# A fused attention and convolution layer: the part behind the softmax in tiles of 128 tokens, with another route for the attention output and another prologue

## The chip, the cores and the metric

One core of a Trainium2 chip runs the whole layer in one launch. The metric is the device time of one run in microseconds (us). Three runs of the kernel before took 492.2, 495.87 and 496.88 us; their median is 495.87 us.

## The reference

Input x holds 64 samples of 64 channels by 1024 values; to the attention part each sample is 64 tokens of 1024 features. Cut to what matters:

```
h   = gelu(gelu(cond@W0+b0)@W1+b1); att = softmax(h@W2+b2)          # [64, 8]
y   = (att . weight)[b, 64, 64] @ x[b] + att@bias_k                  # mixes the 64 tokens of a sample
q   = y@Wq + bq  (32 x 32 heads);  k = y@Wk + bk;  v = y@Wv + bv     # k, v: [.., 32]
p   = softmax(q * k / sqrt(32)) per token, 32 x 32;  o = p @ v, but only [.., 32] values a token
x1  = x + o, each value of o repeated 32 times
u   = conv1d(x1, 64->64 channels, 9 taps, 4 groups, pad 4) + ctx(cond) + bias
out = x1 + u @ W4bit.T + bias
```

The reshape of the kernel uses that o is broadcast over the heads: q has to be known only as its sum over heads for the broadcast values, so Wq, Wk and Wv together give 96 columns (`w3`).

## The kernel before

The 64 samples go in 16 **units** of four (256 tokens), and a unit has two halves of 128 tokens. Per unit:

1. `project` multiplies x of the unit with `w3` (f32), ScalarE copies z to SBUF (`z_copy`), `mix` applies the mixing matrix of each sample; VectorE makes the softmax of 32 x 32 per token in `scores` and `attend`, half by half, and writes o in `divide` (L601).
2. SyncE writes o to DRAM for each half (`save_o`, L247) and, when both halves are there, reads it back eight times in the layout of the convolution, 16 partitions a time (`spread_o`, L254), in pieces of 32 values (128 bytes).
3. GpSimd adds it to the convolution's input (`add_o`: three instructions for each of four channel groups, L327, L328, L330), ScalarE takes the upper part in the reduced f32 format (`c_high`, L410), GpSimd the rest (`c_low`, L336). TensorE makes the convolution of a group with six matmuls of 512 columns (`conv`, L709).
4. ScalarE adds the bias (`u_copy`, L419), TensorE transposes (`transpose_u`), ScalarE and VectorE split again (`u_high`, L427; `u_low`, L605).
5. `linear` multiplies with the 4-bit weights: 64 matmuls of 512 columns a unit, in 16 slots of four. VectorE adds x1 (`finish`, L613; x1 comes from GpSimd's `residual`), SyncE stores.

Each engine runs a list written out by hand and waits on semaphores. In iteration i TensorE makes `linear` of unit i-2 and, in fixed slots between, `conv` and `transpose_u` of unit i-1, and `project` and `mix` of unit i+1. ScalarE, VectorE, GpSimd and SyncE have their own lists in the same iterations. Everything that SyncE issues goes through one queue, in order.

Ahead of the loop lies a prologue: a small network gives `att`; 64 matmuls with 24 rows make the mixing matrices (L784; the weights are split in two parts by VectorE L483, L486 and GpSimd L306); sums over the heads give `w3` (L514); units 1 to 4 are projected ahead (`NZ` = 5). The projection of unit 0 is L794, column sums are L798.

Of the kernel before, what the change touches and what calls it, by code (L numbers as in the profile page):

```python
# [13 lines left out]
P = 128  # L14
# [8 lines left out]
UT = UB * S  # L23
NU = B // UB
NT = NU * TU
SLOTS = 16
# [11 lines left out]
for _name, _n in (("cond", B), ("w0", P), ("w1", P), ("w2", KE), ("b0", 1), ("b1", 1), ("cbias", G), ("part", 1),  # L38
                  ("scale", 1), ("zero", 1), ("b2", KE), ("mixb", P), ("brow", W3)):
    AT[_name] = slice(NCOLS, NCOLS + _n)  # L40
    NCOLS += _n


def block_program(nc, xt_in, xc_in, cols, mix_w, wq, wvk, conv_w, ctx_w, packed_t, xn_in, bias_in, out):
    ctx = ExitStack()
    with ctx:
# [15 lines left out]
        xc = sb("xc", [P, 2, UB, G, MW])  # L62
        c_hi = sb("c_hi", [P, UB, G, MW], F32R)
# [11 lines left out]
        o_sb = sb("o_sb", [P, 2, TU, DH])  # L75
        o_c = sb("o_c", [P, 2, UB, G, DH])
        u_sb = sb("u_sb", [P, 2, UB * P])
# [15 lines left out]
        cond_sb, w0_sb, w1_sb, w2_sb, b0_sb, b1_sb, cbias_sb, part_sb, sc, zero, b2_all, mixb_all, brow_all = (  # L93
            cols_sb[:, at] for at in AT.values())
        b2_sb = b2_all[0:B, :]
        mixb_sb = mixb_all[0:2 * KE, :]
        brow_sb = brow_all[0:NH, :]
        h_sb = sb("h_sb", [P, 2, B])
        att = sb("att", [B, 3, KE])
        att_s = sb("att_s", [B, 4])  # L100
        att_r = sb("att_r", [B, 4, DH], F32R)
        att_t = sb("att_t", [P, B], F32R)
        mix_bias = sb("mix_bias", [P, NT])
        u_bias = sb("u_bias", [P, G, B])
        zp = sb("zp", [P, 5])
# [6 lines left out]
        mixw = prob[:, 0, :, :].rearrange("p d e -> p (d e)")  # L112
        mixw_hi = c_hi[:, :, :, :].rearrange("p n g m -> p (n g m)")[:, 0:D]
        mixw_r = c_lo[:, :, :, :].rearrange("p n g m -> p (n g m)")[:, 0:2 * D].rearrange("p (s h i) -> p s h i", h=2, i=S)
# [25 lines left out]

        o_dram = nc.dram_tensor("o_dram", [NU, UT, DH], F32).ap()

# [22 lines left out]
        s_mwh = sem("s_mwh")  # L165
        s_mwr = sem("s_mwr")
        s_mwd = sem("s_mwd")
# [8 lines left out]
        s_zp = sem("s_zp")  # L176
        s_flag = sem("s_flag")
# [19 lines left out]
        s_x1 = sem("s_x1")  # L197
# [13 lines left out]
        def ut_view(t, b, g):  # L211

            return t[:, b % 2, :, :].rearrange("p r (n g c) -> p g n r c", n=UB, g=G)[:, g, :, :, :]


        NI = NU + 3

        Z_SLOT = (1, 6)
        CONV_SLOT = (3, 5, 8, 10)
        UT_SLOT = (7, 9, 11, 12)  # L220
        MIX_SLOT = 13
# [3 lines left out]
        def _(eng):  # L225
# [10 lines left out]
            def load_c(u):  # L236
                if u >= 2:
                    eng.wait_ge(s_cl, G * (u - 1))
                eng.dma_start(xc[:, u % 2, :, :, :], xc_in[u]).then_inc(s_xc[u % 2], 16)

            def store(d, t):
                eng.wait_ge(s_res, 4 * d + 2 * t + 2)
                eng.dma_start(out[d, t], xn[:, d % NXN, t, :]).then_inc(s_out[d % NXN], 16)

            def save_o(a, t):
                eng.wait_ge(s_o, TU * a + t + 1)
                eng.dma_start(o_dram[a, t * P:(t + 1) * P, :], o_sb[:, a % 2, t, :]).then_inc(s_ow, 16)  # L247
# [16 lines left out]
            eng.dma_start(cw[:, :, :, :], conv_w).then_inc(s_cw, 16)  # L264
            load_c(0)
            eng.dma_start(ctx_sb[:, :, :], ctx_w).then_inc(s_ctx, 16)
            eng.wait_ge(s_w3[0], 1)
            load_x(1)
            load_x(2)
            load_c(1)  # L270
            for u in range(3, NZ):
                load_x(u)
            eng.dma_start(bias_n[:, :], bias_in).then_inc(s_bias, 16)

            for i in range(NI):
                a, d = i, i - 2
                if 0 <= d - 1 < NU:
                    store(d - 1, 1)
                if NZ <= i + 2 < NU:
                    load_x(i + 2)  # L280
                if a < NU:
                    save_o(a, 0)
                if 2 <= i + 1 < NU:
                    load_c(i + 1)
                if a < NU:
                    save_o(a, 1)
                    spread_o(a)
# [10 lines left out]
        def _(eng):  # L298
            eng.memset(att_r[:, :, :].bitcast(F32), 0.0).then_inc(s_zero, 1)
# [5 lines left out]
            eng.wait_ge(s_mwr, 1)  # L305
            eng.tensor_copy(mixw_r[:, :, 1, :], mixw_r[:, :, 0, :].bitcast(F32)).then_inc(s_mwd, 1)  # L306
# [9 lines left out]
            def add_o(b, g):  # L316


                x4 = xc[:, b % 2, :, g, 1:MW].rearrange("p n (d j) -> p n d j", j=4)
                x0 = xc[:, b % 2, :, g, 0:P].rearrange("p n (d j) -> p n d j", j=4)  # L320
                o = o_c[:, b % 2, :, g, :]
                if g == 0:
                    eng.wait_ge(s_xc[b % 2], 16 * (b // 2 + 1))
                    eng.wait_ge(s_oc[b % 2], 16 * R * (b // 2 + 1))  # L324
                else:
                    eng.wait_ge(s_add, 3 * (G * b + g))
                eng.tensor_tensor(x4[:, :, :, 0:3], x4[:, :, :, 0:3], o.unsqueeze(3).broadcast_to([P, UB, DH, 3]), ALU.add).then_inc(s_add, 1)  # L327
                eng.tensor_tensor(x4[0:64, :, :, 3], x4[0:64, :, :, 3], o[0:64], ALU.add).then_inc(s_add, 1)  # L328
                eng.wait_ge(s_add, 3 * (G * b + g) + 1)
                eng.tensor_tensor(x0[64:P, :, :, 0], x0[64:P, :, :, 0], o[64:P], ALU.add).then_inc(s_add, 1)  # L330

            def c_low(b, g):
                eng.wait_ge(s_add, 3 * (G * b + min(g + 2, G)))
                eng.wait_ge(s_ch, G * b + g + 1)
                eng.wait_ge(s_conv, G * (b - 1) + g + 1)
                eng.tensor_tensor(c_lo[:, :, g, :], xc[:, b % 2, :, g, :], c_hi[:, :, g, :].bitcast(F32), ALU.subtract).then_inc(s_cl, 1)  # L336

            def residual(b, t):
                if t == 0:
                    eng.wait_ge(s_add, 3 * G * (b + 1))  # L340
                    eng.wait_ge(s_xn[b % NXN], 16 * (b // NXN + 1))
                    if b == 0:
                        eng.wait_ge(s_bias, 16)
                x = xn[:, b % NXN, t, :]
                runs = x.rearrange("p (d e) -> p d e", d=DH)
                eng.wait_ge(s_o, TU * b + t + 1)
                eng.tensor_tensor(runs, runs, o_sb[:, b % 2, t, :].unsqueeze(2).broadcast_to([P, DH, D // DH]), ALU.add).then_inc(s_x1, 1)  # L347
                eng.wait_ge(s_x1, 4 * b + 2 * t + 1)
                eng.tensor_tensor(x, x, bias_n[:, :], ALU.add).then_inc(s_x1, 1)  # L349

            for b in range(NU):
                add_o(b, 0)
                add_o(b, 1)
                if b:
                    c_low(b, 0)
                add_o(b, 2)
                if b:
                    c_low(b, 1)
                add_o(b, 3)
                if b:  # L360
                    c_low(b, 2)
                    c_low(b, 3)
                residual(b, 0)
                residual(b, 1)
# [3 lines left out]
        def _(eng):  # L368
            for n, bias in enumerate((b0_sb, b1_sb)):
                eng.wait_ge(s_pe0, n + 1)  # L370
                eng.activation(h_sb[:, n, :], p_sm[0][:, 64 * n:64 * n + 64], ACT.Gelu, bias=bias).then_inc(s_act0, 1)
            eng.wait_ge(s_att, 3)
            eng.activation(att[:, 1, :], att[:, 0, :], ACT.Exp, accum_out=att_s[:, 2:3]).then_inc(s_act0, 1)
            for m in range(8):
                eng.wait_ge(s_mixed, m + 1)
                for h in range(2):
                    rows = slice(h * S, h * S + S)
                    eng.activation(mix_t[rows, :, 8 * m:8 * m + 8].rearrange("p t s -> p s t"),
# [517 lines left out]
```

## Time and profile before

| | |
|---|---|
| Median of three runs | 495.87 us (492.2 to 496.88) |
| Profiled execution | 494.59 us |
| Its span, first to last instruction | 492.8 us |
| Busy in the span: TensorE, VectorE, ScalarE, GpSimd | 450.7, 333.2, 228.3, 346.8 us |
| Instructions | 7038 |
| Moved by DMA | 79.78 MB in 55522 packets, 41904 of them under 512 bytes |

All durations below come from the one profiled execution. A matmul in f32 leaves two records, one in the reduced format leaves one. Records of matmuls overlap, so their cost is read from start to start, not from their length.

### The profile page before, as it was taken

The page shows a single profiled execution, that of the slowest core. Times are in us where ns is not written, and L with a number is a line of the kernel's source. Part 1 is how long each engine was busy: PE and PEld are TensorE (multiplying, and loading weights), DVE is VectorE, ACT ScalarE, POOL GpSimd, SP SyncE. Part 2 cuts the span into 40 slices and gives each one's busy share as a digit, 9 for nine tenths or more (in the row PEclk, how much of TensorE's full clock was granted, in tenths as well). Part 3 has the DMA queues.
Part 4 walks back from the last instruction along what each step waited for, and adds up shares of the span by engine and source line. Part 5 has one row for each costly group of instructions (what it writes and reads, how often), then busy time and mean ns, then how long its engine had stood idle before and what let it go on. Part 6 is the DMA issues. An engine that isn't in the chain of part 4 may idle for free. (4 is left out here: it accounts for less than half of the span.)

```text
span 492.8 us, 7038 instructions
## 1 busy us (share of the span) xinstructions
PE 450.7 (91%) x2403; PEld 373.5 (76%) x2403; DVE 333.2 (68%) x532; ACT 228.3 (46%) x458; POOL 346.8 (70%) x329
## 2 busy tenths in 40 slices
PE   3998272999999999999999999999999999997996
PEld 2998151777877888888888888787888888775885
DVE  4639685739793968677785949495968678692121
ACT  2705570546354545545463645454544535472520
POOL 2400493969697968797696969697869788696920
PEclk9999596799999999999999999999999999999999
DMA  8956324254555556473827464546547352606112
GB/s 338 413 212 217 106 89 108 65 132 184 139 224 142 221 133 235 116 252 97 269 97 214 149 171 161 150 175 163 200 116 252 106 178 93 190 4 189 47 44 85
DMA packets 55522, 79.78 MB, mean 162 GB/s; under 512 B 41904, under 2 KB 41904, under 8 KB 50864
## 3 DMA queue, kind: packets, MB, share of 16 engines
q1 hardware_dynamic: 55472, 79.08, 49.7%
q8 instruction: 35, 0.57, 0.5%
q14 instruction: 15, 0.12, 0.1%
HBM read 61.76 MB, written 17.30 MB: 160 GB/s over the span
## 5 line engine op out<-in xcount | busy, mean ns | idle before, releaser
L725 PE MATMUL p_f<-w_ffn,u_lo 128*128 128x512 f32 x512 | 204.1, 399 | 0.0
L725 PE MATMUL p_f<-w_ffn,u_hi 128*128 128x512 f32 x512 | 202.2, 405 | 1.1 <-DVE u_lo L605 1.1
L419 ACT ACTIVATE u_sb<-p_conv,u_bias,cols_sb 128x128 f32<-128x128 f32 x256 | 96.2, 457 | 59.9 <-PE p_conv L709 59.0
L327 POOL TENSOR_TENSOR xc<-xc,o_c 128x384 f32<-128x384 f32 x64 | 56.7, 886 | 92.2 <-DMA o_c<-o_dram 90.8
L725 PEld LDWEIGHTS p_f<-w_ffn,u_hi 128*128 128x128 f32 x512 | 97.0, 189 | 21.2 <-issue 1.3
L725 PEld LDWEIGHTS p_f<-w_ffn,u_lo 128*128 128x128 f32 x512 | 97.1, 190 | 18.3
L613 DVE TENSOR_TENSOR xn<-p_f,xn 128x512 f32<-128x512 f32 x64 | 44.0, 688 | 84.5 <-PE p_f L725 84.5
L336 POOL TENSOR_TENSOR c_lo<-xc,c_hi 128x516 fp32r<-128x516 f32 x60 | 78.3, 1310 | 9.7 <-issue 6.2
L410 ACT ACTIVATE c_hi<-xc 128x516 fp32r<-128x516 f32 x64 | 40.8, 638 | 87.6 <-POOL xc L330 87.5
L349 POOL TENSOR_TENSOR xn<-xn,bias_n 128x1024 f32<-128x1024 f32 x32 | 77.1, 2408 | 2.5
L709 PE MATMUL p_conv<-c_hi,cw_hi 128*128 128x512 f32 x128 | 53.6, 419 | 26.0 <-POOL c_lo L336 14.6
L605 DVE TENSOR_TENSOR u_lo<-p_ut,u_hi 128x512 fp32r<-128x512 f32 x64 | 43.9, 689 | 33.0 <-ACT u_hi L427 32.9
L347 POOL TENSOR_TENSOR xn<-xn,o_sb 128x1024 f32<-128x1024 f32 x32 | 61.7, 1928 | 0.1
L709 PE MATMUL p_conv<-c_lo,cw_hi 128*128 128x512 f32 x128 | 52.5, 410 | 0.0
L709 PE MATMUL p_conv<-c_hi,cw_lo 128*128 128x512 f32 x128 | 52.4, 410 | 0.0
L709 PEld LDWEIGHTS p_conv<-c_hi,cw_hi 128*128 128x128 f32 x128 | 24.9, 194 | 35.4 <-issue 29.6
L427 ACT ACTIVATE u_hi<-p_ut 128x512 fp32r<-128x512 f32 x64 | 38.6, 603 | 26.6 <-PE p_ut L720 25.2
L404 ACT ACTIVATE prob<-prob 128x1024 f32<-128x1024 f32 x32 | 34.0, 1062 | 30.3 <-DVE prob L580 30.3
L686 PEld LDWEIGHTS p_sm<-w,xt 128*128 128x128 f32 x384 | 46.3, 191 | 1.8
L686 PE MATMUL p_sm<-w,xt 128*128 128x96 f32 x384 | 46.0, 273 | 0.0
L584 DVE TENSOR_REDUCE den<-prob 128x32 f32<-128x1024 f32 x32 | 38.7, 1210 | 7.3 <-ACT prob L404 7.3
L592 DVE TENSOR_REDUCE p_sm<-prob 128x32 f32<-128x1024 f32 x32 | 39.3, 1228 | 1.1
(99 smaller groups left out, 502.5 us busy)
## 6 DMA issues: line engine op xcount, KB each, us to landing
xc<-xc_in_in SPq DMA_DIRECT2D x16, 1032.0 KB, 5.0
xt<-xt_in_in SPq DMA_DIRECT2D x16, 1024.0 KB, 7.6
xn<-xn_in_in SPq DMA_DIRECT2D x16, 1024.0 KB, 6.0
out<-xn SPq DMA_DIRECT2D x32, 512.0 KB, 6.5
o_c<-o_dram SPq DMA_DIRECT2D x128, 32.0 KB, 2.1
xn<-wq_in SPq DMA_DIRECT2D x3, 1024.0 KB, 10.6
xt<-wq_in SPq DMA_DIRECT2D x1, 1024.0 KB, 6.5
prob<-mix_w_in SPq DMA_DIRECT2D x1, 512.0 KB, 4.4
```

Source lines behind the costliest of these rows:

```text
L327: eng.tensor_tensor(x4[:, :, :, 0:3], x4[:, :, :, 0:3], o.unsqueeze(3).broadcast_to([P, UB, DH, 3]), ALU.add).then_inc(s_add, 1)
L336: eng.tensor_tensor(c_lo[:, :, g, :], xc[:, b % 2, :, g, :], c_hi[:, :, g, :].bitcast(F32), ALU.subtract).then_inc(s_cl, 1)
L347: eng.tensor_tensor(runs, runs, o_sb[:, b % 2, t, :].unsqueeze(2).broadcast_to([P, DH, D // DH]), ALU.add).then_inc(s_x1, 1)
L349: eng.tensor_tensor(x, x, bias_n[:, :], ALU.add).then_inc(s_x1, 1)
L410: eng.activation(c_hi[:, :, g, :], xc[:, b % 2, :, g, :], ACT.Copy).then_inc(s_ch, 1)
L419: ins = eng.activation(u_sb[:, g % 2, n * P:(n + 1) * P], p_conv[g % 2][:, n * P:(n + 1) * P], ACT.Identity, bias=u_bias[:, g, UB * b + n: ...
L592: eng.tensor_reduce(num(a)[:, t, :], prob[:, t, :, :], AX.X, ALU.add).then_inc(s_num, 1)
L605: eng.tensor_tensor(ut_view(u_lo, b, g), p_ut[g % 2][:, :].rearrange("p (n r c) -> p n r c", n=UB, r=R), ut_view(u_hi, b, g).bitcast(F32), ...
L613: eng.tensor_tensor(x, p_f[q % 2][:, :], x, ALU.add).then_inc(s_res, 1)
L686: last = mm(z_ps(a)[:, t * W3:(t + 1) * W3], xt[:, a % NXT, r, t * P:(t + 1) * P], w3[:, r, :], start=(r == 0), stop=(r == R - 1))
L709: last = mm(p_conv[g % 2][:, :], w[:, k, g, :], src[:, :, g, k:k + P], start=(n == 0), stop=(n == 5))
L725: return mm(p_f[half][:, :], u[:, d % 2, r, t * P:(t + 1) * P], w_ffn[:, r, 512 * half:512 * half + 512], **flags)
```

## The change

A **tile** k is half a unit: 128 tokens, two samples; there are 32, and two of them share a buffer of a unit.

- Behind the softmax everything goes by tiles: `add_o`, `c_high`, `c_low`, `conv`, `u_copy`, `transpose_u`, `u_high`, `u_low`, `linear`, `finish`. `conv` has six matmuls of 256 columns (48 a unit, not 24), `transpose_u` two transposes and not four, `linear` the same matmuls as before in 8 slots a tile.
- VectorE writes o four times over (`o_sb` [.., 32, 4]); `save_o` and `spread_o` run once a tile, and the spread moves runs of 128 values (512 bytes), shifted by one column for the first 64 partitions. `add_o` becomes one instruction a group. There are 256 issues of `spread_o`, not 128, of 64 KB and not 32.
- The mixing matrices come from plain f32: 128 matmuls with 8 rows, on four groups of 32 rows, and no split on VectorE and GpSimd. ScalarE's queue loads their weights (4 DMAs).
- The prologue's order is another: column sums between the projections of unit 0 chunk by chunk, `u_bias` on ScalarE, weights of the linear part converted in four pieces, `keep_busy` matmuls of a matrix of ones (6, three times 4, and 16).
- GpSimd adds the bias and o to x in the other order (`x_bias`, `x_o`), and makes `c_low` of unit 0 too.

In the diff the loops over `NU + 2`, `NT + 1`, `NT` and `NT` are those of SyncE, GpSimd, ScalarE and VectorE, in this order.

```diff
-SLOTS = 16
+SLOTS = 8
-        o_sb = sb("o_sb", [P, 2, TU, DH])
+        o_sb = sb("o_sb", [P, 2, TU, DH, 4])
+        def conv_slot(k, g):
+            return SLOTS * k - 8 + g if k < 6 else SLOTS * k - 12 + 2 * g
+        def ut_slot(k, g):
+            return SLOTS * k - 6 + g if k < 6 else SLOTS * k - 9 + 2 * g
+        PROJ = {2 * SLOTS * (a - 3) + 3 + 4 * t: (a, t) for a in range(NZ, NU) for t in range(TU)}
+        MIX = {2 * SLOTS * (a - 3) + 13: a for a in range(3, NU)}
...
             def spread_o(k):
+                t = k % TU
+                eng.wait_ge(s_ow, 16 * (k + 1))
...
                 for r in range(R):
+                    at = 1 if r < PAD else 0
+                    eng.dma_start(o_c[r * CG:(r + 1) * CG, TN * t:TN * t + TN, :, at:at + P].rearrange("c n g m -> c (n g) m"),
+                                  o_dram[k].rearrange("(q c) m -> c q m", c=CG)).then_inc(s_oc[t], 16)
...
+            for i in range(NU + 2):
+                if 0 <= 2 * i - 4 < NT:
+                    store(2 * i - 4)
+                if 2 <= i < NU:
+                    load_c(i)
+                if 1 <= i < NU:
...
+                    load_n(i)
+                if i < NU:
+                    save_o(2 * i)
+                    spread_o(2 * i)
+                    save_o(2 * i + 1)
+                    spread_o(2 * i + 1)
...
+                x = rows_of(xc[:, (k // TU) % 2, :, :, :], k, g)
+                eng.tensor_tensor(x, x, rows_of(o_c, k, g), ALU.add).then_inc(s_add, 1)
...
+            for k in range(NT + 1):
+                if k < NT:
+                    add_o(k, 0)
+                    add_o(k, 1)
+                    c_low(k, 0)
+                    add_o(k, 2)
+                    c_low(k, 1)
+                    add_o(k, 3)
+                    c_low(k, 2)
+                    c_low(k, 3)
+                if k >= 1:
+                    if k >= 3:
+                        x_bias(k - 1)
+                    x_o(k - 1)
...
+            for k in range(NT):
+                a, t = k // TU + 1, k % TU
+                nxt = k + 1 < NT
+                if t == 0 and 2 <= a < NU:
+                    exp(a, 0)
+                u_copy(k, 0)
+                c_high(k, 3)
+                u_copy(k, 1)
+                u_high(k, 0)
+                if t == 0 and a < NU:
+                    exp(a, 1)
+                if nxt:
+                    c_high(k + 1, 0)
+                u_copy(k, 2)
...
+            for k in range(NT):
+                a, t = k // TU + 2, k % TU
+                A, N = a < NU, k + 1 < NT
+                if k:
+                    finish(k - 1, 1)
+                if N:
+                    u_low(k + 1, 0)
+                if A and t == 0:
+                    softmax_top(a)
+                    score(a, 0)
+                if A and t == 1:
+                    sum_exp(a, 0)
+                    times_v(a, 0)
+                if N:
+                    u_low(k + 1, 1)
+                if A and t == 0:
+                    subtract(a, 0)
+                if A and t == 1:
+                    sum_v(a, 0)
+                    divide(a, 0)
+                finish(k, 0)
...
+            def keep_busy(bank, n):
+                for _ in range(n):
+                    mm(bank[:, 0:P], ones[:, :], ones[:, :], start=True, stop=True)
...
+            for n in range(CG):
+                for j in range(4):
+                    rows = slice(32 * j, 32 * j + KE)
+                    for h in range(2):
+                        last = mm(p_mixed[j][h * S:h * S + S, NT * n:NT * n + NT], mixw[rows, n, :], att_t[rows, h::2], start=True, stop=True)
...
+            keep_busy(p_f[1], 16)
+            conv(0, 0)
...
+            for s in range(SLOTS * NT):
+                linear(s // SLOTS, s % SLOTS)
+                if s in TRANS:
+                    k, g = TRANS[s]
+                    transpose_u(k, g)
+                if s in CONV:
+                    k, g = CONV[s]
+                    conv(k, g)
```

**Where instructions moved.** TensorE in the middle of the loop. Before, a group's convolution between two slots of `linear`, and its transposes (L709, L720; L725 is `linear`):

```order
L709 MATMUL p_conv<-c_hi,cw_hi 128x512 [waits s_cl,s_u]
L709 MATMUL p_conv<-c_lo,cw_hi 128x512
L709 MATMUL p_conv<-c_hi,cw_lo 128x512
L709 MATMUL p_conv<-c_hi,cw_hi 128x512
L709 MATMUL p_conv<-c_lo,cw_hi 128x512
L709 MATMUL p_conv<-c_hi,cw_lo 128x512
L725 MATMUL p_f<-w_ffn,u_hi 128x512
L725 MATMUL p_f<-w_ffn,u_lo 128x512
L725 MATMUL p_f<-w_ffn,u_hi 128x512
L725 MATMUL p_f<-w_ffn,u_lo 128x512
L720 MATMUL p_ut<-ident,u_sb 128x128 [waits s_ul,s_u]
L720 MATMUL p_ut<-ident,u_sb 128x128 x3
```

Now the same place of the list (L722, L731; L736 is `linear`):

```order
L722 MATMUL p_conv<-c_hi,cw_hi 128x256 [waits s_cl,s_u]
L722 MATMUL p_conv<-c_lo,cw_hi 128x256
L722 MATMUL p_conv<-c_hi,cw_lo 128x256
L722 MATMUL p_conv<-c_hi,cw_hi 128x256
L722 MATMUL p_conv<-c_lo,cw_hi 128x256
L722 MATMUL p_conv<-c_hi,cw_lo 128x256
L736 MATMUL p_f<-w_ffn,u_hi 128x512
L736 MATMUL p_f<-w_ffn,u_lo 128x512
L736 MATMUL p_f<-w_ffn,u_hi 128x512
L736 MATMUL p_f<-w_ffn,u_lo 128x512
L731 MATMUL p_ut<-ident,u_sb 128x128 [waits s_ul,s_u]
L731 MATMUL p_ut<-ident,u_sb 128x128
```

A group comes twice as often, with half the columns and half the transposes; its waits come twice as often too.

ScalarE in the loop. Before, the upper parts of the next unit (L410, c_hi) stand in a block ahead of the copies of u (L419) of the same unit:

```order
L410 ACTIVATE c_hi<-xc 128x4x129 [waits s_conv,s_add] x2
L404 ACTIVATE prob<-prob 128x1024 [waits s_sub]
L410 ACTIVATE c_hi<-xc 128x4x129 [waits s_conv,s_add]
L419 ACTIVATE u_sb<-p_conv,u_bias,cols_sb 128x128 [waits s_ut,s_conv]
L419 ACTIVATE u_sb<-p_conv,u_bias,cols_sb 128x128 x3
```

Now c_hi (L421) of tile k+1 stands between the copies (L429) and the upper parts (L437) of tile k:

```order
L429 ACTIVATE u_sb<-p_conv,u_bias,cols_sb 128x128 [waits s_ut,s_conv]
L429 ACTIVATE u_sb<-p_conv,u_bias,cols_sb 128x128
L437 ACTIVATE u_hi<-p_ut 128x2x8x16 [waits s_f,s_ut]
L421 ACTIVATE c_hi<-xc 128x2x129 [waits s_conv,s_add]
L429 ACTIVATE u_sb<-p_conv,u_bias,cols_sb 128x128 [waits s_ut,s_conv]
L429 ACTIVATE u_sb<-p_conv,u_bias,cols_sb 128x128
L437 ACTIVATE u_hi<-p_ut 128x2x8x16 [waits s_f,s_ut]
L421 ACTIVATE c_hi<-xc 128x2x129 [waits s_conv,s_add]
```

So a wait for `add_o` of the next tile now stands ahead of the third and fourth `u_copy` of this one.

## Rows read from the trace of the kernel before

**Rows 1.** The page, parts 1 and 2: busy us, share, instructions; slices in tenths

```profile
PE 450.7 (91%) x2403; PEld 373.5 (76%) x2403; DVE 333.2 (68%) x532; ACT 228.3 (46%) x458; POOL 346.8 (70%) x329
...
PEclk9999596799999999999999999999999999999999
...
GB/s 338 413 212 217 106 89 108 65 132 184 139 224 142 221 133 235 116 252 97 269 97 214 149 171 161 150 175 163 200 116 252 106 178 93 190 4 189 47 44 85
```

**Rows 2.** Waits of TensorE from 60 us on: us in total, times, longest

```profile
PE p_conv L709 <- POOL c_lo L336: 14.6, 3, 10.6
```

**Rows 3.** Timeline of TensorE, 0 to 75 us: start, us, engine, line, names

```profile
11.26 2.96 PE L784 MATMUL p_ut<-att_t,c_lo 24*128 24x64 f32 x13
...
22.54 6.21 PE L794 MATMUL p_conv<-w,xt 128*128 128x96 f32 x32
28.58 1.95 PE L798 MATMUL p_sm<-w,ones 128*128 128x96 f32 x16
31.37 0.55 PE L697 MATMUL p_sm<-z_sb,mix_t 64*64 64x96 f32 x8 [0.83 <-ACT z_sb L396]
...
32.78 3.76 PE L686 MATMUL p_sm<-w,xt 128*128 128x96 f32 x32
...
58.80 0.76 PE L709 MATMUL p_conv<-c_hi,cw_hi 128*128 128x512 f32 x1 [10.05 <-DVE c_lo L617]
...
72.70 0.47 PE L725 MATMUL p_f<-w_ffn,u_hi 128*128 128x512 f32 x1 [1.14 <-DVE u_lo L605]
```

**Rows 4.** Timeline of TensorE, 74 to 115 us

```profile
87.43 0.77 PE L709 MATMUL p_conv<-c_hi,cw_hi 128*128 128x512 f32 x1 [10.60 <-POOL c_lo L336]
```

**Rows 5.** The chain that ended last: start us, us, what

```profile
441.11 1.41 DMA o_dram<-o_sb
...
446.66 2.29 DMA o_c<-o_dram
...
454.59 2.90 PE p_conv L709 x6
...
459.25 1.46 PE p_conv L709 x6
460.71 2.08 PE p_f L725 x9
...
489.08 0.69 DVE xn L613
```

**Rows 6.** Timeline of VectorE, 0 to 110 us

```profile
6.42 1.29 DVE L486 SCALAR_TENSOR_TENSOR c_lo<-c_hi,cols_sb,prob 128x1024 fp32r<-128x1024 f32 x1
...
32.53 0.23 DVE L561 TENSOR_TENSOR k_sb<-p_sm,qkv_bias 128x64 f32<-128x64 f32 x1
...
42.57 0.19 DVE L601 TENSOR_TENSOR o_sb<-p_sm,rden 128x32 f32<-128x32 f32 x1
...
46.76 0.19 DVE L601 TENSOR_TENSOR o_sb<-p_sm,rden 128x32 f32<-128x32 f32 x1
...
96.93 0.19 DVE L601 TENSOR_TENSOR o_sb<-p_sm,rden 128x32 f32<-128x32 f32 x1
```

**Rows 7.** Timeline of GpSimd, 0 to 120 us

```profile
107.34 0.89 POOL L327 TENSOR_TENSOR xc<-xc,o_c 128x384 f32<-128x384 f32 x1 [3.47 <-DMA o_c<-o_dram]
```

**Rows 8.** Groups by line and shape: busy us, mean ns; idle before

```profile
L419 ACT ACTIVATE u_sb<-p_conv,u_bias,cols_sb 128x128 f32<-128x128 f32 x256 | 96.2, 457 | 59.9 <-PE p_conv L709 59.0
L336 POOL TENSOR_TENSOR c_lo<-xc,c_hi 128x516 fp32r<-128x516 f32 x60 | 78.3, 1310 | 9.7 <-issue 6.2
...
L327 POOL TENSOR_TENSOR xc<-xc,o_c 128x384 f32<-128x384 f32 x64 | 56.7, 886 | 92.2 <-DMA o_c<-o_dram 90.8
...
L605 DVE TENSOR_TENSOR u_lo<-p_ut,u_hi 128x512 fp32r<-128x512 f32 x64 | 43.9, 689 | 33.0 <-ACT u_hi L427 32.9
L410 ACT ACTIVATE c_hi<-xc 128x516 fp32r<-128x516 f32 x64 | 40.8, 638 | 87.6 <-POOL xc L330 87.5
...
L330 POOL TENSOR_TENSOR xc<-xc,o_c 64x128 f32<-64x128 f32 x64 | 33.7, 526 | 4.8
```

More of the change, by code:

```diff
@@ L156, in block_program @@
         s_ow = sem("s_ow")
-        s_oc = [sem(f"s_oc{i}") for i in range(2)]
+        s_oc = [sem(f"s_oc{t}") for t in range(TU)]
         s_ident = sem("s_ident")
@@ L351, in _ @@
[L351 to L364, printed above, removed]
+                    eng.wait_ge(s_xc[(k // TU) % 2], 16 * (k // (2 * TU) + 1))
+                    eng.wait_ge(s_oc[k % TU], 16 * R * (k // TU + 1))
@@ L438, in _ @@
+            convert_weights(1, 0)
+            exp(0, 1)
+            convert_weights(1, 1)
+            for a in range(1, NZ):
+                z_copy(a)
+            eng.wait_ge(s_ub, G)
+            c_high(0, 0)
             exp(1, 0)
-            c_high(0, 0)
-            exp(1, 1)
             c_high(0, 1)
-            u_copy(0, 0)
             c_high(0, 2)
-            u_copy(0, 1)
-            u_high(0, 0)
-            c_high(0, 3)
-            u_copy(0, 2)
-            u_high(0, 1)
-            u_copy(0, 3)
@@ new lines, in _ @@
+            for k in range(NT):
[19 more added lines that the diff above has]
+                finish(k, 0)
+                if N:
+                    u_low(k + 1, 2)
+                if A and t == 0:
+                    score(a, 1)
+                if A and t == 1:
+                    sum_exp(a, 1)
+                    times_v(a, 1)
+                if N:
+                    u_low(k + 1, 3)
+                if A and t == 0:
+                    subtract(a, 1)
+                if A and t == 1:
+                    sum_v(a, 1)
+                    divide(a, 1)
@@ L735, in linear, with product, open_bank @@
-            def linear(d, slot):
-                q, n = slot // 4, slot % 4
+            def product(k, half, r, u, **flags):
+                t = k % TU
+                return mm(p_f[half][:, :], u[:, (k // TU) % 2, r, t * P:(t + 1) * P], w_ffn[:, r, 512 * half:512 * half + 512], **flags)
+            def open_bank(k, half):
+                if k:
+                    eng.wait_ge(s_res, 2 * k + half - 1)
+                product(k, half, 0, u_hi, start=True, stop=False)
+            def linear(k, slot):
+                half, n = slot // 4, slot % 4
@@ L760, in linear @@
-                if n == 3 and q == 1:
-                    open_bank(d, 2)
+                        product(k, half, r, u_lo, start=False, stop=True).then_inc(s_f, 1)
             eng.wait_ge(s_small, 16)
@@ L807, in _ @@
             last.then_inc(s_cb, 1)
-            for a in range(1, NZ):
+            for a in range(2, NZ):
                 for t in range(TU):
```

543 lines of the change are left out of this document (228 added, 315 removed).

## The prediction, made before the changed kernel had run

> **What bounds the kernel now.** I read the page first, then TensorE's timeline, its waits, and the chain. The page shows TensorE busy for 450.7 us of 492.8, VectorE for 333.2, GpSimd for 346.8 [rows 1]. From 87 us on TensorE hardly waits: the loop is bound by the matmuls. What is not matmul lies at three places. Ahead of the loop: the first convolution comes at 58.80, the first matmul of `linear` at 72.70 [rows 3]. A hole of 10.60 us before 87.43, where TensorE waits for GpSimd's `c_low` of unit 1 [rows 4]. One of about 3.4 us near the end, of the same kind (14.6 us in three waits) [rows 2]. The chain shows what lies behind such a wait: o saved, spread, added on GpSimd, split, then `conv` at 454.59 [rows 5]. After a hole the granted clock is at its lower level, 1.2 GHz (the slices with 5, 9, 6 [rows 1]): six matmuls of a convolution take 2.90 us there, 1.46 us at 2.4 GHz [rows 5].
>
> The profiled run took 494.59 us, 1.8 more than its span; the median of the three is 1.3 above it. I sum the span and carry both over.
>
> **The change part by part: until the softmax of unit 0 starts** (k_sb at 32.53 [rows 6]). The mixing matmuls start at 11.26 [rows 3], after VectorE has been held by the splitting (6.42 to 7.7 [rows 6]). Without that, `att` is ready 2 us earlier: start 9.2. They took 11.3 us (to 22.54). Now 128 f32 matmuls make 256 passes. Bounds: all 64-column weight loads one after the other at 1.2 GHz; the 16 passes of L798, each with a load of 128 columns, took 1.95 us at the higher level, .12 each [rows 3]; 64 columns at half the clock take about as much, 256 x .11 = 28 us. Or four row groups side by side, a quarter of that: 7 us. `mix`, whose halves lie on two row groups, makes eight passes of 64 columns in .55 us, .069 each at 2.4 GHz [rows 3]; with four groups at 1.2 GHz the same per pass or somewhat less. I take 10 us, near the low end, as that row has row groups too: end 19.2. Then 48 passes of unit 0 and column sums, and 24 of `keep_busy`. Passes with 128-column weights took 6.21/32 = .194 in L794 and 3.76/32 = .117 in L686 [rows 3]: the clock rose in between. 72 passes are 8.4 us at the one, 14 at the other level; before, 48 took 8.0. I take 10: 29.2, then 1.2 to the softmax, as before less the bias that is now made earlier: **start at 30.4**, 2.1 earlier.
>
> **From there to the first `linear`** (before: 72.70-32.53 = 40.2). Times from the softmax's start. o of tile 0 is ready at 10.3 (42.76), of tile 1 at 14.5 (46.95) [rows 6]. Before, the spread waited for both. Now tile 0 goes at once: save 1.4, eight issues 3.9, landing 2.3 [rows 5], 2.5 us of waiting behind `load_x(4)`, issued just before (1 MB at the 413 GB/s of the busiest slice [rows 1]), and .3, my guess for twice the bytes: o lands at 20.7. `add_o` was 886 ns for 384 elements, `c_low` 1310 for 516 [rows 8]: about 2.2 ns an element over .2 us, so .75 each for 258. `c_low(0,0)` ends at 23. TensorE itself comes at 25: three projections of .113 x 32 = 3.6 us, each behind its load, then 16 `keep_busy`, 3.6. Then the groups pass through ScalarE: `u_copy` .75 (96.2 us over 256, two each), `c_high` .4 (638 ns for 516 elements) [rows 8], two `exp` of 1.05, in an order in which `c_high(1,g)` of tile 1 stands between. o of tile 1 lands at 26, as its save waits for tile 0's eight issues; GpSimd, through with `c_low(0,3)` at 27.8, adds it by 28.6. Stepwise on ScalarE: `c_high(1,0)` 29.5, `u_copy(0,2)` 30.2, `u_copy(0,3)` 31.7, last `u_high` 32.9, and VectorE's `u_low` 33.3. **`linear` starts at 33.4**, 6.8 sooner; in all at 63.8 instead of 72.70.
>
> **The loop.** Before: 489.08-72.70 = 416.4 us [rows 3, 5]. Off: holes 14.6 [rows 2] and matmuls at half clock, 11 x .2 + 1.44 = 3.6. That leaves 398.2. Added:
> - Conv: a 512-column matmul takes 1.46/6 = .243 [rows 5], of which 512/2.4 GHz is .213, so .03 besides. With 256 columns: .107+.03 = .137; `linear`'s .231 (2.08 us for nine) gives .124. I take .130: 48 x .130 - 24 x .243 = +.41 a unit, 15 units: **+6**. Over the 744 conv matmuls of tiles 1 to 31 the bounds are .113 (L686's 32 starts spread over 3.6 us, weights of 128 columns and a short stream), -12.6; and .22 (L686's pass and a 256-column stream in turn), +67.
> - Tile 1's convolution and transposes lie now behind the first `linear`: 24 x .13 + 8 x .11 (a pass of L686) = **+4**.
> - Transposes: as many as before, side by side with nothing lost in a switch: 0.
> - New waits. `u_copy(k,2)` stands behind `c_high(k+1,0)`. Early on, tiles 2 and 4 arrive late for it: o of tile 2 is divided at 31.7 (behind `u_low(0,1)`, 31.05), plus 8.5 for save and spread (as above, with no load ahead) 40.2, plus add, upper part and copy 42.1; the transposes are due at 40, after four slots of 1.42 (.92 of `linear`, half a conv group's .78, .11). **+2.2**. Tile 4: `u_low(2,0)` after slot 10 of `linear`, 51.9, then `attend` (4.2, as from 42.57 to 46.76 [rows 6]): divided 56.4, copy ready 66.8, due 64.9: **+2**. Tile 6 is just in time. Later see rival C. With 1.8 for the last units, whose slots are shorter: **+6** in all.
> - VectorE: u_low 128 x .42 instead of 43.9, the wider o .1 x 32: +13 us, to about 346. GpSimd: one add of .75 replaces 886 and two of about 530 ns, -28; `c_low` +18. Both stay below 85% and hide behind TensorE.
> - SyncE: 128 more issues of .45 and a dozen MB more; the queue idles for most of a unit. 0, but see C.
>
> Loop 398.2+6+4+6 = 414.2, and 3.7 from 489.08 to the end for the last add and store, as before. **Span 30.4+33.4+414.2+3.7 = 481.7**, run 483.5, against a median 484.8: I say **484.5**.
>
> **A rule against the change.** The rows first. In L686 load and stream of 96 columns take .117 together [rows 3], and the stream is .04 of it (96/2.4 GHz) if each column takes a cycle, .08 if two; so a load of 128 columns takes .04 to .08 of its own at least, and in turn with 512 columns' .213 it would make .25 to .29. The nine `linear` matmuls, each with a fresh weight, take .231 [rows 5]: the load hides. The Trainium skill ("TensorE: Matmul & The Clock Gate", "The mechanism" in Part 3) says that a weight load overlaps running matmuls only when its row group differs. By that rule load and stream of a conv matmul come in turn; taken from the rows, that is the .22 above at most, and 484.5+67 = 551. The rows contradict it; chance .02. The same page ("Back-to-back issue gap") gives 262 cycles for 256 columns, .109 us; it would make 484.5-16 = 469, the far end of A below. Its 518 cycles for 512 (.216) are less than this trace's .231 and .243.
>
> **The rivals.**
> A, 476: tiles arrive in time everywhere (-4) and conv goes at the .124 of the `linear` row (-4.5). For it: the two stalls of 2 us hang on sums of a dozen terms, in which I put each transfer behind its longest neighbour. Against: `c_high` stands where it does. Chance .24.
> B, 497: the mixing matmuls don't run side by side. At two groups' pace they take 18 to 28 us, not 10, and the whole prologue follows, +8 to +18. Against: `mix` shows two at a time. Chance .12.
> C, slower, 508: each even tile j. VectorE can divide its o only after `u_low(j-2,1)`, whose transposes come in slot 8j-23; `u_copy(j-1,2)`, behind `c_high(j,0)`, must be ready for slot 8j-13. Ten slots are 10 x 4 x .231 + 5 convolutions of .78 + transposes 1.1 + a projection 1.8 + `mix` .55 = 16.6 us. In them must pass 2.9 (split, sum, divide), save to arrival, and 1.95 (add, `c_high`, `u_copy`): room for 11.7 us. Save to arrival was 7.8 in the chain (441.11 to 448.95 [rows 5]) and 10.2 (97.12 to 107.34 [rows 6, 7]). Now it has twice the bytes and stands behind a store and two loads, 2.5 MB. From 11.7 on every us is paid in 13 units: at 13.5, 1.8 x 13 = +23. Chance .14.
> Weight loads in turn: 551, .02. The forecast, 478 to 491: .48.
>
> **The numbers.** A measurement of this kernel can tell about 1%, 491 to 501 around 495.87. Faster by over 1%: nearly all of the forecast (.46) and A (.24) = .70. Within: B and the forecast's rest, .14. Slower: C and the loads, .16. The range reaches from A's low end, 473, to where C begins, 499: it leaves out C, the loads and little of A.
>
> **What would show it.** The first `linear` matmul at 64 us, not 73; no hole of 10 us after it, but two of about 2; conv matmuls .124 to .137 apart; mixing matmuls over in about 10 us; the o transfer within 11.7 us of `divide`. Wrong if TensorE waits for u_sb in every second tile, if the mixing takes over 15 us, or if the conv matmuls are .15 or more apart.

## The result: 25.7% slower, not 2% faster

The changed kernel took **621.78 us** (median of four runs, 619.83 to 623.82) beside 494.93 us for the kernel before on the same chip. The ratio is 1.257, its 95% interval 1.249 to 1.265. The profiled span is 620.6 us, the forecast was 481.7. Forecast, range and sign were wrong. One rival (C) had the kernel slower, at 508 us by a late o; none names what happened.

First the page of the changed kernel, parts 1, 2 and 6 (engine, busy us, share, instructions; the slices; then the DMA issues with KB each and median us to landing). It answers to [rows 1].

```profile
PE 486.8 (78%) x3047; PEld 421.0 (68%) x3047; DVE 329.5 (53%) x584; ACT 227.9 (37%) x579; POOL 330.4 (53%) x333
...
PEclk9989898987969979698796977969879698899999
...
o_c<-o_dram SPq DMA_DIRECT2D x256, 64.0 KB, 2.6
```

GpSimd is down from 346.8 to 330.4 us and VectorE is near its old value: no engine has become the bound. But TensorE is busy for 78% only, and its clock falls again and again over the whole run, where before it stayed up from the ninth slice on. Next, what TensorE waits for from 60 us on (us in total, times, longest), against the single line of [rows 2]:

```profile
PE p_sm L699 <- DMA xt<-xt_in_in: 95.6, 11, 9.7
PE p_sm L710 <- ACT z_sb L410: 7.7, 11, 0.8
PE p_ut L731 <- ACT u_sb L429: 7.2, 6, 2.0
PE p_f L736 <- DVE u_lo L608: 6.0, 5, 1.9
```

`project` waits for x in 11 places, units 5 to 15, each time nearly 9 us. One of them, on SyncE's queue (start, us, line, names):

```profile
314.50 0.33 SPq L260 DMA_DIRECT2D o_dram<-o_sb  x1
316.93 3.64 SPq L271 DMA_DIRECT2D o_c<-o_dram  x8
320.61 0.43 SPq L260 DMA_DIRECT2D o_dram<-o_sb  x1
323.19 4.92 SPq L271 DMA_DIRECT2D o_c<-o_dram  x8
328.15 0.43 SPq L256 DMA_DIRECT2D out<-xn  x1
328.62 0.43 SPq L241 DMA_DIRECT2D xt<-xt_in_in  x1
344.24 0.34 SPq L256 DMA_DIRECT2D out<-xn  x1
```

and on TensorE (the first projection of that unit, and the second, 16 passes each):

```profile
334.23 3.73 PE L699 MATMUL p_sm<-w,xt 128*128 128x96 f32 x16 [8.71 <-DMA xt<-xt_in_in]
...
343.53 1.92 PE L699 MATMUL p_sm<-w,xt 128*128 128x96 f32 x16
```

TensorE is ready for x at 334.23 - 8.71 = 325.52. SyncE issues the load only at 328.62, as its list now has `load_x(i + 2)` as the last thing of an iteration, behind both tiles' `save_o` and `spread_o` and a store. In the kernel before it was the second thing of an iteration, behind one store and ahead of both saves; the bullets on the change don't list this move. x can be used 5.6 us after the issue. 3.1 late + 5.6 = 8.7 us. And the 16 passes behind the hole take 3.73 us, the 16 a little later 1.92: TensorE comes out of the hole at the lower clock, 1.2 GHz (granted .50 from 334 to 338 us). The stretches of 20 us of the same trace (busy us of TensorE, granted clock, DMA share, GB/s):

```profile
320.00:340.00 20.00, 11.29 (x59) 0.74 0.39 120
340.00:360.00 20.00, 19.30 (x121) 1.00 0.47 165
```

### The profile page after: what moved, and what is told of

It reads as the page before. It is cut to its first block and busy times, and to the rows that moved or that the text cites. A ratio compares the mean times of both kernels' runs of the same rounds, so it can differ in the third digit from the quotient of the medians.

```text
span 620.6 us, 9085 instructions
## 1 busy us (share of the span) xinstructions
PE 486.8 (78%) x3047; PEld 421.0 (68%) x3047; DVE 329.5 (53%) x584; ACT 227.9 (37%) x579; POOL 330.4 (53%) x333
## 5 line engine op out<-in xcount | busy, mean ns | idle before, releaser
L344 POOL TENSOR_TENSOR c_lo<-xc,c_hi 128x258 fp32r<-128x258 f32 x128 | 95.4, 745 | 236.8 <-ACT c_hi L421 232.7
L736 PE MATMUL p_f<-w_ffn,u_hi 128*128 128x512 f32 x512 | 208.2, 417 | 6.0 <-DVE u_lo L608 6.0
L736 PE MATMUL p_f<-w_ffn,u_lo 128*128 128x512 f32 x512 | 209.4, 410 | 0.0
L608 DVE TENSOR_TENSOR u_lo<-p_ut,u_hi 128x256 fp32r<-128x256 f32 x128 | 53.7, 420 | 241.3 <-ACT u_hi L437 240.4
L699 PE MATMUL p_sm<-w,xt 128*128 128x96 f32 x384 | 66.0, 344 | 95.6 <-DMA xt<-xt_in_in 95.6
L437 ACT ACTIVATE u_hi<-p_ut 128x256 fp32r<-128x256 f32 x128 | 49.6, 388 | 195.6 <-PE p_ut L731 195.0
L429 ACT ACTIVATE u_sb<-p_conv,u_bias,cols_sb 128x128 f32<-128x128 f32 x256 | 102.9, 457 | 46.6 <-PE p_conv L722 46.6
L736 PEld LDWEIGHTS p_f<-w_ffn,u_hi 128*128 128x128 f32 x512 | 99.1, 194 | 21.0 <-DVE u_lo L608 6.5
L736 PEld LDWEIGHTS p_f<-w_ffn,u_lo 128*128 128x128 f32 x512 | 100.7, 197 | 12.5
L338 POOL TENSOR_TENSOR xc<-xc,o_c 128x258 f32<-128x258 f32 x128 | 93.8, 744 | 18.0 <-DMA o_c<-o_dram 18.0
L421 ACT ACTIVATE c_hi<-xc 128x258 fp32r<-128x258 f32 x128 | 54.7, 427 | 104.6 <-POOL xc L338 104.6
L722 PE MATMUL p_conv<-c_hi,cw_hi 128*128 128x256 f32 x256 | 75.2, 294 | 0.0
L722 PE MATMUL p_conv<-c_lo,cw_hi 128*128 128x256 f32 x256 | 73.8, 288 | 0.0
L722 PE MATMUL p_conv<-c_hi,cw_lo 128*128 128x256 f32 x256 | 73.5, 287 | 0.0
L731 PE MATMUL p_ut<-ident,u_sb 128*128 128x128 f32 x256 | 50.0, 277 | 7.5 <-ACT u_sb L429 7.4
L722 PEld LDWEIGHTS p_conv<-c_hi,cw_hi 128*128 128x128 f32 x256 | 50.3, 196 | 5.6
L731 PEld LDWEIGHTS p_ut<-ident,u_sb 128*128 128x128 f32 x256 | 35.3, 142 | 27.1 <-ACT u_sb L429 10.9
L722 PEld LDWEIGHTS p_conv<-c_lo,cw_hi 128*128 128x128 f32 x256 | 50.0, 195 | 5.2
```

Of the source, the lines that this page charges most:

```text
L338: eng.tensor_tensor(x, x, rows_of(o_c, k, g), ALU.add).then_inc(s_add, 1)
L344: eng.tensor_tensor(rows_of(c_lo, k, g), rows_of(xc[:, (k // TU) % 2, :, :, :], k, g), rows_of(c_hi, k, g).bitcast(F32), ALU.subtract).the ...
L421: eng.activation(rows_of(c_hi, k, g), rows_of(xc[:, (k // TU) % 2, :, :, :], k, g), ACT.Copy).then_inc(s_ch, 1)
L429: ins = eng.activation(u_sb[:, g % 2, n * P:(n + 1) * P], p_conv[g % 2][:, n * P:(n + 1) * P], ACT.Identity, bias=u_bias[:, g, bat:bat + 1 ...
L437: eng.activation(ut_view(u_hi, k, g), p_ut[g % 2][:, 0:TN * P].rearrange("p (n r c) -> p n r c", n=TN, r=R), ACT.Copy).then_inc(s_uh, 1)
L608: eng.tensor_tensor(ut_view(u_lo, k, g), p_ut[g % 2][:, 0:TN * P].rearrange("p (n r c) -> p n r c", n=TN, r=R), ut_view(u_hi, k, g).bitcas ...
```

## The experiments

Two theories of the 127 us. **T1**: the place of `load_x` in SyncE's list. **T2**: o's transfers, of four times the bytes, crowd the queue or the memory, so that x comes late wherever it is issued. (Expectations name them so.)

**x_early: the load of x at the head of the iteration.**

```diff
             for i in range(NU + 2):
+                if NZ <= i + 2 < NU:
+                    load_x(i + 2)
                 if 0 <= 2 * i - 4 < NT:
                     store(2 * i - 4)
...
-                if NZ <= i + 2 < NU:
-                    load_x(i + 2)
```

> The changed kernel with one edit: SyncE issues load_x(i+2) at the head of iteration i, ahead of the store, not at its end. Theory 1, the place in the queue: in the changed kernel the load is issued behind both spreads and lands 8 to 9.7 us after TensorE wants it, in each of 11 units. Then the edit takes away the 95.6 us of waiting and the matmuls at half clock behind them (about 25 us): 480 us, between 474 and 490. Theory 2, the transfers of o crowd the DMA queue with four times the bytes, so that x is late wherever it is issued: the wait moves or shrinks by less than half, 560 us or more, or o becomes late in its stead.

Measured: 499.48 us beside 494.74, ratio 1.010 (1.007 to 1.013), span 495.8. TensorE's waits from 60 us on, the one for x gone:

```profile
PE p_sm L710 <- ACT z_sb L410: 7.7, 11, 0.8
PE p_ut L731 <- ACT u_sb L429: 7.3, 7, 2.0
PE p_f L736 <- DVE u_lo L608: 6.0, 5, 1.9
```

Moving one DMA a unit is worth 122.3 us. That is T1; but the expectation for the kernel without this fault was 480, at most 490, and it still lies 1% on the wrong side of the kernel before.

**x_mid: the load between the two halves' o.** The same two lines behind `spread_o(2 * i)`, ahead of `save_o(2 * i + 1)`.

> The same load between the two halves of the o transfer (behind spread_o(2i), ahead of save_o(2i+1)). Theory 1: it is issued about 5 us earlier than in the changed kernel, at the end of the first spread, and lands at about the time that TensorE wants it: 480 to 500 us, and o of the odd tiles 2 to 3 us later at no cost, since they have room. Theory 2: as with the load early, over 560 us.

Measured: 500.39 us, ratio 1.014 (1.007 to 1.022); TensorE waits 2.1 us for x in five places, at most .9. The edge lies here: the load may stand behind one half's o, not behind both.

**before_x_late: the kernel before, with the changed kernel's place of the load** (behind `spread_o` and `store(d, 0)`).

> The kernel before with only the place of the load changed as in the change: load_x(i+2) at the end of SyncE's iteration, behind spread_o and store. Theory 1: there it is issued at about slot 13 of 16, lands 7 us later, and is wanted in slot 1 of the next iteration: 1 to 3 us late in each of 11 units, 10 to 35 us slower, 505 to 530 us. Theory 2 (bytes): the spread has its old bytes, so no change, 495 us.

Measured: 562.41 us, ratio 1.138 (1.131 to 1.145). Its trace:

```profile
PE p_sm L686 <- DMA xt<-xt_in_in: 41.2, 11, 8.1
PE p_conv L709 <- POOL c_lo L336: 12.1, 2, 8.7
```

Here o moves as it did before, in 128 pieces of 32 KB, and the same 11 waits come in, one of 8.1 us and ten of 2.8 to 4.3. T2 isn't needed. Nor is x's load slower beside o's larger transfers: the loads of x land 6.8 us after their issue in the changed kernel (median), 9.1 us here. The waits of the changed kernel are longer because more of the list lies ahead of the load: from the first save of an iteration to the load 14.1 us there (314.50 to 328.62), 10.7 here (220.07 to 230.77).

The late load cost 68 us where I had expected at most 35: the waits for x are 41.2 of it, so some 27 us are something else. The granted clock is .918 instead of .971. Times the spans that is 46.1 - 14.3 = 32 us of full-speed time, an estimate and an upper one, as TensorE idles for a part of it: enough for the rest.

**after_no_x: the changed kernel without the x loads of units 5 to 15** (old data is projected; the 11 MB are not moved).

```diff
-                if NZ <= i + 2 < NU:
-                    load_x(i + 2)
...
-                    eng.wait_ge(s_x[a % NXT], 16 * (a // NXT + 1))
+                    eng.wait_ge(s_x[a % NXT], 16 * (min(a, NZ - 1 - (NZ - 1 - a) % 2) // NXT + 1))
```

> The changed kernel without the x loads of units 5 to 15; it leaves out these transfers (11 MB) and projects old data, all else as it is. Theory 1: the time without any wait for x, 478 us, within 1% of the early load. Theory 2: if the o transfers themselves are late for the convolution, some of the loss stays: over 500 us.

Measured: 497.18 us in one run, span 495.4, against the early load's 495.8. As far as one run can tell, an early x costs nothing, by its bytes or its place. Theory 1's 478 us did not come in: what is left above it has another cause than x.

### What the idle holes cost beside their length

The span fell by 124.8 us with the early load, the waits for x were 95.6; 29.2 us are left. **after_fill** has 70 extra matmuls in each hole, on the changed kernel with its late load:

```diff
                 if t == 0:
+                    if a >= NZ:
+                        eng.wait_ge(s_o, TU * (a - 1))
+                        keep_busy(z_ps(a), 70)
                     eng.wait_ge(s_x[a % NXT], 16 * (a // NXT + 1))
```

> The changed kernel with its late x load, and 70 extra f32 matmuls of ones (128 columns, into the bank that the projection then overwrites) ahead of project's wait for x in units 5 to 15: TensorE stays busy in the hole of about 9 us. Their results are not used. At the .11 us a pass of the row of transposes 70 of them fill about 7.7 us of it. Theory 1 (the stretch at 1.2 GHz comes from the idle hole, and costs 20 to 29 us in all 11 units beside the 95.6 of waiting): the lower level behind the holes goes, and the time falls from 622 to 593 to 603 though more work is done. Rival (the clock would fall there anyway, or its fall costs nothing that the next wait for x doesn't take back): 615 to 625.

Measured: 670.05 us, at a granted clock of .986 instead of .89. Both ranges were missed, as I had taken a matmul of ones for one pass. It leaves two:

```profile
305.65 15.79 PE L689 MATMUL p_sm<-ones 128*128 128x128 f32 x140
321.29 1.92 PE L702 MATMUL p_sm<-w,xt 128*128 128x96 f32 x16
```

15.6 us are more than the hole, and TensorE never waits for x. So **fill_36** has 36 of them.

> As the run with 70 extra matmuls ahead of the late x of units 5 to 15, but 36 of them. The 70 were two passes each, .112 us apart (112 records in 12.51 us), 15.7 us a unit, more than the hole; its span was the early load's 495.8 and 11 x 15.7 = 172.7 more, 668.5 (669.1 measured), at a granted clock of .986. 36 fill 8.1 of the 8.7 us that TensorE waits on average: 88.7 of the 95.6. Theory 1 (the lower clock comes from the idle hole): only waits are filled, so no time is added, and what the stretches at 1.2 GHz cost, about 29 us, goes: span 591 to 595, a median of 593 to 599, with TensorE executing 396 extra matmuls. Rival (the clock costs nothing of its own, the holes are only longer or shorter with it): 620 to 624.

Measured: **594.24 us** (591.63 to 595.5), span 593.7. Waits, and the stretch that answers to the one above:

```profile
PE p_ut L734 <- ACT u_sb L429: 8.5, 8, 2.0
PE p_sm L713 <- ACT z_sb L410: 7.7, 11, 0.8
PE p_sm L702 <- DMA xt<-xt_in_in: 6.6, 6, 1.8
```

```profile
320.00:340.00 20.00, 19.22 (x132) 1.00 0.48 179
```

396 matmuls whose results nobody reads make the kernel 27.5 us faster. x is as late as before, and the clock stays nearly always at its upper level, 2.4 GHz (granted .99 from 100 to 460 us, against .85). Of the span's 26.9 us (620.6 - 593.7) 1.6 lie ahead of the first `linear` (65.02 against 63.40), so 25.3 come from the loop; x_early gives 29.2 for the same thing. So the 127 us over the kernel before are: waits for x 95.6, the clock's fall behind them 25 to 29, and 2 to 6 that have to do with neither.

### The rest: two places in ScalarE's list

At x_early's `mix` TensorE waits for `z_copy` once a unit. ScalarE's timeline of that kernel shows why (start, us, line, names, idle before):

```profile
150.04 0.38 ACT L437 ACTIVATE u_hi<-p_ut 128x256 fp32r<-128x256 f32 x1 [1.72 <-PE p_ut L731]
150.32 0.32 ACT L410 ACTIVATE z_sb<-p_sm 128x192 f32<-128x192 f32 x1
```

The copy stands behind the last `u_high`, which waits for transposes that TensorE has just issued, right ahead of `mix`. **z_early** puts it in front of `u_copy(k, 3)`; **chigh_late** moves the two `c_high` behind `u_copy`; **both** does both:

```diff
+                u_copy(k, 2)
                 if nxt:
                     c_high(k + 1, 0)
-                u_copy(k, 2)
                 u_high(k, 1)
+                if t == 0 and NZ <= a + 1 < NU:
+                    z_copy(a + 1)
+                u_copy(k, 3)
                 if nxt:
                     c_high(k + 1, 1)
-                u_copy(k, 3)
                 u_high(k, 2)
                 if nxt:
                     c_high(k + 1, 2)
                 u_high(k, 3)
-                if t == 0 and NZ <= a + 1 < NU:
-                    z_copy(a + 1)
```

> The early x load, and ScalarE's z_copy of the next unit put ahead of u_copy(k,3) instead of at the end of the unit's list, behind u_high(k,3). In the profile with the x load early TensorE waits 7.7 us in 11 places at mix for that z_copy. Theory 1 (the copy stands behind u_high, which waits for transposes that TensorE issues in the slot of mix itself): those 7.7 us go, and the time falls from 499.5 to 492, range 489 to 495; the waits for u_sb and u_lo stay at 7 and 6 us. Rival (the waits change place, as u_copy is now behind z_copy, .3 us later): u_sb's wait grows by 5 us or more and the time stays within 2 us of 499.5.

Measured: 495.07 us beside 494.02, ratio 1.002 (1.000 to 1.005). The 7.7 us at `mix` are gone, but u_sb's wait grew:

```profile
PE p_ut L731 <- ACT u_sb L429: 10.7, 14, 2.0
PE p_f L736 <- DVE u_lo L608: 6.7, 6, 1.9
```

Theory and rival each had a half: of the 7.7 us, 3.4 came back at u_sb and .7 at u_lo, and the time lies just outside the range of the one (489 to 495) and the condition of the other.

> The early x load, and on ScalarE c_high(k+1,0) behind u_copy(k,2) and c_high(k+1,1) behind u_copy(k,3), each one place later than in the changed kernel. TensorE waits 7.3 us at the transposes for u_sb, which u_copy writes. Theory 1 (u_copy is late because c_high of .43 us waits ahead of it for VectorE or for the addition): the 7.3 us of u_sb and part of the 6.0 us of u_lo behind it go, and the time falls from 499.5 to 492 to 496. Rival (u_copy waits for the convolution, or c_high, later now, holds up c_low and the next convolution): a new wait of TensorE at conv for c_hi or c_lo of 5 us or more, and a time from 499 to 506.

Measured: 495.52 us, ratio 1.005 (1.004 to 1.007). The time is within theory 1's range, but u_sb's wait only fell by half, to 3.9 us in four places, and u_lo's rose to 7.4. The rival's new wait of 5 us didn't come; `conv` waits .5 us for u_sb.

> Both edits of ScalarE's list on top of the early x load. If the two waits are independent the gains add up: 499.5 less 7.7 less 4 to 7 is 485 to 488, range 483 to 492, under the kernel before by 1 to 2%. Rival (one wait stands behind the other, and VectorE's finish and u_low set the pace of the unit): no more than the better of the two alone, 490 to 493.

Measured: **487.53 us** beside 494.02, ratio .989 (.987 to .991), span 485.5. The gain of 12.0 us on x_early is more than the two alone (4.4 and 4.0). x_early ran on another chip; by the ratios, each to its own kernel before, the gains are 2.1% against .8 and .5%, so this holds. The waits behave alike: 8.5 us less in all, against 3.6 and 1.5. It fits that with `c_high` out of the way the early `z_copy` no longer pushes `u_copy` back (u_sb's wait is 4.0 us, not 10.7), but no run tests this reason by itself:

```profile
PE p_f L736 <- DVE u_lo L608: 7.4, 6, 2.2
PE p_ut L731 <- ACT u_sb L429: 4.0, 5, 1.1
PE p_conv L722 <- ACT u_sb L429: 1.1, 3, 0.6
```

### The keep_busy matmuls

> The early x load, and none of the keep_busy matmuls (6 ahead of the mixing, 4 at three places between the sums of Wq, 16 ahead of the first convolution). Theory 1 (they fill waits and hold nothing up): the lower clock of 1.2 GHz comes in for 3 to 7 us at one or two more places of the first 60 us, and the time is 0 to 4 us over 499.5. Rival (they lie on the path themselves): 1 to 3 us less than 499.5.

Measured: 493.50 us, ratio 1.001 (.999 to 1.004), runs from 492.63 to 497.03. That is 6.0 us under x_early, on another chip, where at most 3 had been expected. Not all of it is in the trace: in the profiled execution (496.91 us) the first `linear` comes at 62.36 instead of 65.33, but the span is only .7 us shorter, 495.1. The first matmuls of the loop run at the lower clock (granted .52 from 61 to 68 us, against .85 in x_early), as theory 1 had said they might, and the waits in the loop are 1.1 us longer. With so wide a spread this decides nothing, so the next runs take them out of `both`, with `both` beside it on the same chip.

> Early x load, both edits of ScalarE's list, and no keep_busy matmuls. In the run with the x load early, taking them out gave 493.5 against 499.5, of which the two batches' spread may be a part. If they lie on the path: 482 to 486. If that difference was chance: 487 to 489, as with both edits alone.

> Early x load and both edits of ScalarE's list once more, for a closer ratio to the kernel before: 487 to 488.5, ratio .986 to .991.

Measured: both_nb **482.19 us** (ratio .979, .976 to .982), both_again 487.14 us (.988, .985 to .990). The first `linear` matmul of each, both_again first:

```profile
65.70 0.47 PE L736 MATMUL p_f<-w_ffn,u_hi 128*128 128x512 f32 x1 [1.36 <-DVE u_lo L608]
```

```profile
59.78 0.47 PE L736 MATMUL p_f<-w_ffn,u_hi 128*128 128x512 f32 x1 [1.37 <-DVE u_lo L608]
```

They hold the prologue up by 5.9 us, and the span of 485.7 falls to 479.4. The 68 passes take 10.9 us in all, so they lie on the path for about half of their time: the twelve ahead of the mixing (which starts at 9.4 without them, 10.5 with them), the eight ahead of a chunk of Wq (three times) and the 32 ahead of the first convolution stand where less than their length was being waited for. Rows of both_again:

```profile
28.35 1.08 PE L689 MATMUL p_sm<-ones 128*128 128x128 f32 x8
...
54.24 3.84 PE L689 MATMUL p_f<-ones 128*128 128x128 f32 x32
57.83 0.36 PE L722 MATMUL p_conv<-c_hi,cw_hi 128*128 128x256 f32 x1
```

In both_nb the first convolution starts at 51.58, after a wait of 1.77 us for `c_lo`; here the clock doesn't fall behind it (granted 1.00 from 61 to 75 us). This is the fastest version: the change, the load at the head, ScalarE's two moves, and no keep_busy, 2.1% under the kernel before.

## Why the prediction was wrong, step by step

**The step that failed is the bullet on SyncE in the loop**, "128 more issues of .45 and a dozen MB more; the queue idles for most of a unit. 0". It counts the issues that are added and not the one that is moved: `load_x(i + 2)`, from the head of the iteration to its end. A queue that idles for most of a unit still holds an issue until the one ahead is allowed. In the unit shown the save of the even tile waits 7.0 us for `divide`, until 314.50. From there the list is a chain: save, landing, eight issues of `spread_o`, and the same for the odd tile, 14.1 us until the load goes out; the odd tile's own `divide` (over at 319.88) is not waited for. The term put at 0 cost 95.6 us of waits and 25 to 29 us of clock. I compared o's path with its due slot (rival C) and never x's with slot 3 of `project`. What it left out can be read off the changed kernel: TensorE ready at 325.52, the spread over at 328.11, the load issued at 328.62 and of use 5.6 later, 8.7 us, 11 times. I also gave the fall of the clock behind a hole no term for a hole that recurs, though [rows 1, 5] show it.

Rival C looked at the right engine for the wrong transfer. With x early, o of an even tile is saved at 231.11, its eight spreads end at 236.31 and land 2.6 later: 7.8 us, under the 11.7 that it had room for. C didn't come in. Nor did any of the prediction's signs of being wrong come in: they look at u_sb, the mixing and the conv matmuls, none at x.

**Until the first linear: right**, 65.02 against 63.8 (before 72.70).

- Mixing matmuls, taken as 10 us from 9.2: they start at 10.42, behind twelve passes of ones that the sum left out, and the last at 18.4. Eight us, of which 4.11 are one idle stretch that no semaphore explains:

```profile
17.59 0.33 PE L790 MATMUL p_f<-att_t,prob 8*64 8x32 f32 x4 [4.11 <-issue]
```

  So the four row groups do run side by side, faster than the low bound of 7 us without that stretch; B was wrong. The stretch comes behind 200 of the 256 passes here and in x_early, and behind 212 in both_nb and no_busy, where the twelve passes of ones ahead of the mixing are gone: each time at the same place of TensorE's list of instructions, whatever the time. What TensorE lacks there isn't shown.
- Softmax of unit 0 (`k_sb`) at 31.42, forecast 30.4, and 33.6 us from there, forecast 33.4. keep_busy was counted in the sum and never asked what it bought: taken out of `both`, it gives 5 us, more than the whole error of this part.
- `add_o` was taken as .75, measured 744 ns; `c_low` .75, 745 ns; `u_low` .42, 420 ns.

**The loop**, taken as 414.2. With x early it is 492.10 (the last `finish`) - 65.33 = 426.8, 12.6 more:

- Conv, taken as .130 a matmul: .120, as in these rows of the changed kernel:

```profile
57.52 0.28 PE L722 MATMUL p_conv<-c_hi,cw_lo 128*128 128x256 f32 x1
57.64 0.28 PE L722 MATMUL p_conv<-c_hi,cw_hi 128*128 128x256 f32 x1
57.75 0.29 PE L722 MATMUL p_conv<-c_lo,cw_hi 128*128 128x256 f32 x1
57.88 0.29 PE L722 MATMUL p_conv<-c_hi,cw_lo 128*128 128x256 f32 x1
```

  The other side of the term was off as well: a conv matmul before, taken as .243, is .237 (four of them take .95 us, from 201.82 to 202.77, in the kernel before). With .120 and .237 a unit costs 48 x .120 - 24 x .237 = +.07 us, 15 units +1 and not +6: 5 us better than forecast. The rule of the Trainium skill ("TensorE: Matmul & The Clock Gate", "The mechanism") that would have made load and stream come in turn is contradicted once more: taken from the rows, it made .22. The same page's 262 cycles for 256 columns ("Back-to-back issue gap"), .109, is as far below what is measured as my .130 is above.
- New waits, taken as 6. Of x_early's 21.0 us from 60 us on, 2.9 lie ahead of the first `linear` (1.06, .84 and 1.02), so the loop has 18.1, 12.1 more. The early stalls of about 2 us are there (.95 at 79.23, 1.80 at 93.11, 1.96 at 103.32), more of them than two; the 7.7 us of `z_copy` ahead of `mix` were not in the sum. It is a wait of at most .8 us, 11 times, from ScalarE's order alone, and no row of before shows it.
- That leaves 12.6 - 12.1 + 5 = 5.5 us more than forecast. The sum took 3.6 us of lower clock off and put none in, but here too the granted clock falls (.52 from 66 to 69.4 us, .57 from 103 to 107): by these shares about 3 us, an estimate. The rest, 2 to 3 us, stays open.
- VectorE's busy time was forecast at about 346 us and came to 329.5, though `u_low` grew from 43.9 to 53.7 as forecast. VectorE doesn't bound the loop, so this cost nothing.

So of the 137 us between forecast and result 122 are one moved DMA. The other 15 (499.5 against 484.5; 14.1 by the spans, 495.8 against 481.7) are, by the terms above, waits of at most 2.0 us each (+12.1), the start (+1.5), conv (-5), the lower clock (about +3) and what stays open (2 to 3).

## What to carry to other kernels

- In a queue served in order, cost every issue that changes its place, and the wait ahead of it, not the queue's load: for each transfer, when is the latest wait ahead of it over, plus its landing, against the slot of its first reader. A queue that is idle for most of a round was 9 us late here in each of 11 rounds.
- Here an idle hole of TensorE of about 9 us cost 2.3 to 2.7 us more behind it, and holes of 3 to 4 us (before_x_late) also cost more than their length. Matmuls of ones in the hole gave that back; where TensorE was hardly idle 10.9 us of them cost 5.9 (both_again), and what was more than the hole cost its full time (after_fill). So look which of the two a given keep_busy is.
- On an engine whose list holds work of two stages, small moves can work together, as two did here: test them together before dropping either.

## What was not expected of the hardware

- Eleven holes of 8.7 us cost 25.3 us of the loop besides (changed kernel against fill_36), 2.3 a hole: the projection behind one takes 3.73 us instead of 1.92. With matmuls in the holes whose result is never read the granted clock stays at 1.00 in the same stretch.
- 256-column matmuls with a fresh weight each run .120 apart, 512-column ones .233 in the same kernel: per column the short ones cost 3% more, not the 12% of the .130.
- 64 KB in 512-byte runs land in 2.6 us from issue, 32 KB in 128-byte runs in 2.1 (medians); four times the bytes in as many packets a tile did not make x land later here.
- Matmuls of 8 rows on four row groups: 256 passes in 8.0 us, of which 4.1 are one stall, at a fixed place of the instruction list. At .015 us a pass of 32 columns the rest is over four times as fast as `mix` on two groups (.069 with 96 columns [rows 3]), and at the lower clock, going by pace: passes of ones take .24 us ahead of it and .135 at 25.63 (the profile's granted clock reads 1.00 all the way up to there).
